# Pre-LN attention and mixture of experts on one core: the next batch's preparation moved into attention, one job queue on a PSUM bank

## The chip, the core and the metric

One core of a Trainium2 chip (8 on the chip, 7 idle). TensorE (PE), VectorE (DVE), ScalarE (ACT), GpSimd (POOL) and SyncE (SP, which here only starts transfers) each run their own instructions in order, and wait for each other by semaphores. The metric is the time of one execution on the device in microseconds, median of several.

## The reference

Four batches of 512 tokens, 128 columns, f32. With x of shape (4, 512, 128), 16 heads of 8 columns, 8 experts of 512 hidden columns:

```python
def attn(x, Wq, bq, Wk, bk):
    q = (x @ Wq + bq).reshape(B, N, 16, 8).transpose(0, 2, 1, 3)
    k = (x @ Wk + bk).reshape(B, N, 16, 8).transpose(0, 2, 1, 3)
    v = k
    a = softmax(einsum('bhnd,bhmd->bhnm', q, k) * 128 ** -0.5)
    return einsum('bhnm,bhmd->bhnd', a, v).transpose(0, 2, 1, 3).reshape(B, N, C)
def ffn(x, w_gate, W1, b1, W2, b2):
    gate = softmax(x @ w_gate.T)
    scores, idx = top_k(gate, 2)
    cw = (one_hot(idx, 8) * scores[..., None]).sum(axis=1)
    h = gelu(einsum('td,edh->teh', x, W1) + b1, approximate=False)
    return einsum('ted,te->td', einsum('teh,ehd->ted', h, W2) + b2, cw)
x = x + attn(layernorm(x), Wq, bq, Wk, bk)
x = x + ffn(layernorm(x), w_gate, W1, b1, W2, b2)
```

## The kernel before

The order of every engine's work is written out by hand: a loop over the batches b, in it 18 attention slots (SLOTS), then the steps of the expert blocks.

*Preparation of a batch.* VectorE takes the moments of the first norm (ln_moments), GpSimd the inverse square root (inv_sqrt), VectorE applies it (ln_apply). TensorE turns x (turn_x), projects it to q and k (project), VectorE adds the bias (add_bias) into qkf. ScalarE (hi_part) and VectorE (lo_part) split q and k into f16 parts side by side in q_aug and k_aug, 32 columns for each head; v_aug holds v and a column of ones. TensorE turns k and q (turn_k, turn_q); ScalarE copies kT (take_kT), VectorE qT0 (take_qT). SP spreads kT into kTm (spread_k), which holds zero outside a head's 32 rows. All of this goes through the PSUM banks SM0 and SM1, which the score maxima use too.

*Attention.* Per head and 128 tokens one matmul of 512 columns gives the scores (score_max, 64 for a batch) and VectorE reduces them to a negative row maximum (row_max), written into q_aug as one more column. For each group of 4 heads q_aug is turned again with the maxima in it (turn_qr, copied by ScalarE in take_qr), and then scores transposed are computed in pairs (score_pair), ScalarE takes the exponential of two banks at once (L575), and values accumulates over 4 slots into bank AV. turn_out turns the result through bank MISC; VectorE divides by the sum and adds x (x1). Slot s holds score pairs of c = s % 4, group s // 4, and the values of slot s - 1. The maxima of batch b are spread: the first `lead(b)` of them (16, 16, 32, 32) before its attention, the others 4 or 3 a slot (sm_of_slot).

*Between attention b and b + 1.* steps(b) steps: for b = 0 there are 9 with no block in them, for b = 1 and 2 the 15 blocks of batch b - 1, for b = 3 the 30 blocks of batches 2 and 3. A block is 128 slots of one expert: up, gelu on ScalarE, down one step later. The steps also hold the end of the preparation of batch b + 1 with its leading maxima, and the routing of batch b: second norm, turned x2, logits (bank AV), top_two, choose, rank_tokens (bank AV), count_blocks, place, name_blocks. Then GpSimd scatters the tokens (scatter, 8 indirect DMAs), SP loads them (load_slots) and the expert's weights (fetch_weights), and at the end GpSimd gathers and VectorE adds (finish).

```python
        def sm_of_slot(b, s):
            rate = 4 if b <= 1 else 3
            first_m = lead(b) + rate * s
            return list(range(first_m, min(first_m + rate, SM_N)))
```

*The order in a slot on TensorE* (L1040 to L1075): one score maximum, turn_k in the last slot, turn_out, score pair 0, one maximum, score pair 1, two maxima, turn_qr in slots 3, 7 and 11, turn_xg and project in slot 15, values, turn_x in 13, project in 14. A score maximum waits for the row maximum two before it (two banks).

*MISC* holds in turn the turned qr, out, x2 and xg; each has semaphores of its own. q_aug, v_aug, qT0 and kTm exist once. On GpSimd the memsets of kTm and v_aug (L396, L397) stand behind the first inv_sqrt, and the memset of xg (L416), for which SP's filling of xs waits (L295), some way behind them. ScalarE splits W1 into two f16 parts in slots 0 to 7 of batch 0 (split_w1), and GpSimd follows (L420).

## Time and profile before

| | us |
|---|---|
| median of 3 runs | 450.85 (450.57 to 451.21) |
| the profiled execution | 453.28 |
| its span, first to last instruction | 451.5 |
| TensorE busy | 375.0 (83%) |
| VectorE busy | 257.0 (57%) |
| ScalarE busy | 244.9 (54%) |
| GpSimd busy | 110.0 (24%) |
| mean granted TensorE clock | 0.906 of 2.4 GHz |

PE is TensorE's matmuls, PEld its weight loads, L878 is line 878 of the kernel. A row in order of time has the start, the duration, the engine, the line, what is written and read with shapes, how many instructions are merged in it (a merged one's duration reaches from the first start to the last end) and, in brackets, how long the engine had been idle and what ended that. Matmuls overlap, so TensorE's cost is read from start to start. The granted clock is 1.00 at 2.4 GHz and 0.50 at 1.2 GHz; in between it is a mean.

### The profile page before, as it was taken

How to read it: one execution, taken by the hardware profiler on the slowest of the kernel's cores; microseconds unless marked ns; L12 is line 12 of the kernel's file. 1: busy time of each engine (PE TensorE's matmuls, PEld its weight loads, DVE VectorE, ACT ScalarE, POOL GpSimd, SP SyncE). 2: the span in 40 equal slices, each digit the busy share in tenths (PEclk: the TensorE clock that was granted, in tenths of full speed). 3: DMA queues.
4: the chain of work that ended last, by engine and by line, in shares of the span. 5: the costliest groups of instructions: out<-in, count | busy, mean ns of one | idle time of the engine just before them, and what ended most of it. 6: DMA issues, size and time to landing. Idle time of an engine off the chain costs nothing. (4 is left out here: it accounts for less than half of the span.)

```text
span 451.5 us, 8146 instructions
## 1 busy us (share of the span) xinstructions
PE 375.0 (83%) x2858; PEld 208.5 (46%) x2858; DVE 257.0 (57%) x607; ACT 244.9 (54%) x322; POOL 110.0 (24%) x112
## 2 busy tenths in 40 slices
PE   3487889775798889979999898899998999989920
PEld 1232223233122224757833235678532358979910
DVE  7677778646877773467768835477678234000202
ACT  1034889870066658723378789233677874444420
POOL 6911331412600000233043001160150003406133
PEclk8556999995589999989999999899999999999975
DMA  5885000002170000324263001341450012576421
GB/s 178 244 272 148 0 1 1 0 14 57 48 245 0 0 1 1 98 100 157 74 197 112 25 1 36 118 169 59 132 202 23 1 54 86 195 267 210 140 83 52
DMA packets 43875, 42.92 MB, mean 95 GB/s; under 512 B 3314, under 2 KB 33082, under 8 KB 43836
## 3 DMA queue, kind: packets, MB, share of 16 engines
q1 hardware_dynamic: 41788, 38.20, 25.7%
q0 software_dynamic: 2048, 4.20, 3.3%
q8 instruction: 25, 0.41, 0.4%
q14 instruction: 14, 0.11, 0.1%
HBM read 11.58 MB, written 11.01 MB: 50 GB/s over the span
## 5 line engine op out<-in xcount | busy, mean ns | idle before, releaser
L659 DVE TENSOR_REDUCE q_aug<-SM 128x1 f16<-128x512 f32 x240 | 156.5, 690 | 50.1 <-PE SM L878 48.9
L575 ACT ACTIVATE probs<-ST 128x1024 f32<-128x1024 f32 x128 | 125.0, 1022 | 31.6 <-PE ST L923 30.4
L878 PE MATMUL SM<-kTm,qT 128*128 128x512 f16 x240 | 94.9, 409 | 18.6 <-DVE q_aug L659 11.4
L514 ACT ACTIVATE hf<-ST 128x512 f32<-128x512 f32 x60 | 35.6, 597 | 85.5 <-PE ST L987 79.9
L923 PE MATMUL ST<-qT,kTm 128*128 128x512 f16 x256 | 76.3, 388 | 4.1 <-ACT probs L575 3.1
L1003 PE MATMUL ST<-w,hf 128*128 x480 | 67.8, 286 | 1.4 <-ACT hf L514 1.4
L936 PE MATMUL AV<-probs,v_aug 128*32 128x512 f32 x512 | 67.5, 604 | 1.0 <-ACT avs L592 0.9
L878 PEld LDWEIGHTS SM<-kTm,qT 128*128 128x128 f16 x240 | 23.9, 99 | 87.7 <-DVE q_aug L659 71.7
L1003 PEld LDWEIGHTS ST<-w,hf 128*128 128x128 f32 x480 | 59.7, 196 | 4.7 <-issue 2.3
L451 POOL DMA_INDIRECT yg<-ys,pos x32 | 32.5, 1015 | 86.7 <-issue 47.8
L387 POOL TENSOR_TENSOR rstd<-ve,neg_half 128x4 f32<-128x4 f32 x8 | 9.3, 1161 | 157.2 <-DVE ve L631 157.2
L987 PE MATMUL ST<-xgT,wblk 128*128 128x128 f16 x240 | 43.8, 221 | 0.0
L986 PE MATMUL ST<-xgT,wblk 128*128 128x128 f16 x240 | 43.8, 221 | 0.0
L985 PE MATMUL ST<-xgT,wblk 128*128 128x128 f16 x240 | 43.8, 221 | 0.0
L923 PEld LDWEIGHTS ST<-qT,kTm 128*128 128x128 f16 x256 | 23.3, 99 | 38.0 <-ACT probs L575 17.1
L439 POOL DMA_INDIRECT xs<-x2s,pos x32 | 31.6, 989 | 36.8 <-DVE pos L719 28.3
L742 DVE SCALAR_TENSOR_TENSOR res<-yg,wgt,x 128x128 f32<-128x128 f32 x16 | 4.5, 345 | 53.0 <-DMA yg<-ys,pos 53.0
L491 ACT ACTIVATE qT<-MISC 128x512 f16<-128x512 f16 x16 | 9.5, 596 | 39.5 <-PE MISC L905 39.2
L986 PEld LDWEIGHTS ST<-xgT,wblk 128*128 128x128 f16 x240 | 23.7, 99 | 7.2 <-issue 0.3
L985 PEld LDWEIGHTS ST<-xgT,wblk 128*128 128x128 f16 x240 | 23.6, 98 | 2.4
L982 PE MATMUL ST<-sel,wblk 128*128 128x512 f16 x60 | 22.9, 382 | 0.9 <-DMA wblk<-wpk 0.4
L987 PEld LDWEIGHTS ST<-xgT,wblk 128*128 128x128 f16 x240 | 23.7, 99 | 0.0
(133 smaller groups left out, 383.9 us busy)
## 6 DMA issues: line engine op xcount, KB each, us to landing
wblk<-wpk SPq DMA_DIRECT2D x60, 288.0 KB
xs<-xg SPq DMA_DIRECT2D x4, 960.0 KB, 7.3
xg<-xs SPq DMA_DIRECT2D x12, 256.0 KB, 3.2
ys<-ysb SPq DMA_DIRECT2D x12, 256.0 KB, 2.4
w<-L_ffn_W SPq DMA_DIRECT2D x1, 2048.0 KB, 11.3
kTm<-kT SPq DMA_DIRECT2D x32, 64.0 KB, 2.0
xt<-L_attn_x SPq DMA_DIRECT2D x4, 256.0 KB, 3.0
out<-res SPq DMA_DIRECT2D x4, 256.0 KB, 2.2
```

Source lines behind the costliest of these rows:

```text
L439: pool.indirect_dma_start(out=xs[b], out_offset=bass.IndirectOffsetOnAxis(ap=pos[:, b, r, t:t + 1], axis=0), in_=x2s[:, t, :, :].rearrange ...
L451: pool.indirect_dma_start(out=yg[:, t, r, :], out_offset=None, in_=ys[f], in_offset=bass.IndirectOffsetOnAxis(ap=pos[:, f, r, t:t + 1], ax ...
L514: act.activation(hf[:, v % HR, :], UP[v % 2], ACT.Gelu, scale=1.0 / WSCALE).then_inc(gelu_done, 1)
L575: act.activation(probs[:, n % 4, :, :], ST[:, n % 2, :, :], ACT.Exp, scale=SCALE).then_inc(exp_done, 1)
L659: dve.tensor_reduce(q_aug[:, m % 4, m // 4, 24:25], SM[m % 2][:, :], AX.X, ALU.max, negate=True).then_inc(sm_max, 1)
L878: pe.matmul(SM[m % 2][:, :], qT0[:, h // 4, P * (m % 4):P * (m % 4) + P], kTm[:, h // 4, h % 4, :], start=True, stop=True).then_inc(sm_ful ...
L923: mm = pe.matmul(ST[:, n % 2, k % 2, :], kTm[:, g, k, P * c:P * c + P], qT1[:, g % 2, :], start=True, stop=True)
L936: last = pe.matmul(AV[32 * j:32 * j + 32, :], v_aug[:, c, 4 * g + j, :], probs[:, (2 * s + j // 2) % 4, j % 2, :], start=(c == 0), stop=(c ...
L985: pe.matmul(col, wb[:, P * c:P * c + P], xgT[:, gq % 2, j, 0, :], start=False, stop=False)
L986: pe.matmul(col, wb[:, P * c:P * c + P], xgT[:, gq % 2, j, 1, :], start=False, stop=False)
L987: last = pe.matmul(col, wb[:, F + P * c:F + P * c + P], xgT[:, gq % 2, j, 0, :], start=False, stop=(c == HC - 1))
L1003: last = pe.matmul(dst, hf[:, v % HR, P * c:P * c + P], w2[:, bass.ds(expert[v], 1), P * c:P * c + P].rearrange("p a n -> p (a n)"), start ...
```

## The change

1. The preparation of batch 1 and 2 runs inside attention 0 and 1 (slots 0 to 12), that of batch 3 begins at the end of attention 1 and runs in the steps after it. steps(0) is 0; routing of batch 0 moves into slots 0 to 8 of attention 1. q_aug, v_aug, qT0 and kTm become double, xt threefold, with the memsets that this takes; other tensors are laid over one another to make room.
2. Everything but the maxima, scores and values goes through MISC, as numbered jobs (misc_order): a job is filled by TensorE (misc_full) when all jobs before it have been emptied (misc_free). The logits and ranks leave AV, x and the projection, k and q leave SM. In a slot the jobs stand between score pair 1 and the third maximum.
3. The row maxima are one stream over all batches: 16 ahead, then 4 a slot in attention 0 and 1 (none in slots 10 and 11 of attention 1), else 2 a slot or step; batch b + 1's follow batch b's without a pause.
4. Order in a slot on TensorE: maximum, pair 0, maximum, pair 1, jobs, maximum, two values, maximum, two values. qr is turned early in slots 3, 7, 11 for b >= 1, last in the slot for b = 0.
5. For batches 1 to 3 the low parts of q and k are formed on GpSimd and not on VectorE; W1 is split in slots 0, 1, 2, 4, 5, 9, 12, 13, the bias later. The rank moves from step 4 to step 5, name_blocks from 5 to 6. The result is written over x1.

```diff
+        LEAD = 16
+        W_SLOTS = (0, 1, 2, 4, 5, 9, 12, 13)
...
         def steps(b):
-            return max(len(blocks_after(b)) + LAG, 9)
+            return len(blocks_after(b)) + LAG if b else 0
...
+        def misc_of_slot(b, s):
+            p = prep_in_att(b)
+            jobs = []
+            if b == 1 and s == 1:
+                jobs.append(("x2", 0))
+            if p is not None and s == 2:
+                jobs.append(("x", p))
+            if s in QR:
+                jobs.append(("qr", b, QR.index(s)))
+            if b == 1 and s == 3:
+                jobs.append(("lg", 0))
+            if p is not None and s in (4, 5):
+                jobs.append(("pr", p, s - 4))
+            if b == 1 and s == 6:
+                jobs.append(("rk", 0))
+            if s == 6:
+                jobs.append(("out", b, 0))
+            if p is not None and s in (8, 9):
+                jobs.append(("k", p, s - 8))
+            if s == 10:
+                jobs.append(("out", b, 1))
+            if p is not None and s in (10, 12):
+                jobs.append(("q", p, (s - 10) // 2))
+            if s == 14:
+                jobs.append(("out", b, 2))
+            if b >= 1 and s == 15:
+                jobs.append(("xg", NQ * (b - 1)))
+            if s == 17:
+                jobs.append(("out", b, 3))
+            if b == 0 and s == 17:
+                jobs.append(("qr", 1, 0))
+            return jobs
...
+        def misc_of_step(b, i):
...
+            if p is not None and i == 0:
+                jobs.append(("x", p))
+            if i == 2:
+                jobs.append(("x2", b))
+            if i == 3:
+                jobs.append(("lg", b))
+            if p is not None and i in (4, 6):
+                jobs.append(("pr", p, (i - 4) // 2))
+            if i == 5:
+                jobs.append(("rk", b))
+            for v in todo[i:i + 1]:
+                gq = group_of(v)
+                if v == group_first(gq) + 1 and v - 1 + group_len(gq) in todo:
+                    jobs.append(("xg", gq + 1))
...
+        def sm_count_slot(b, s):
+            if b == 0:
+                return 4
+            if b == 1:
+                return 0 if s in (10, 11) else 4
+            return 2
+        def sm_count_step(b, i):
+            return 2 if i < NB and b < B - 1 else 0
...
-            pool.memset(kTm[:, :, :, :], 0.0).then_inc(s_kTm, 1)
-            link(pool.memset(v_aug[:, :, :, :], 0.0))
+            pool.memset(kTm[:, 0, :, :, :], 0.0).then_inc(s_kTm, 1)
+            link(pool.memset(v_aug[:, :, :, :, :].rearrange("p a t h r -> p (a t h r)"), 0.0))
...
             pool.memset(xg[:, :, :], 0.0).then_inc(s_zero, 1)
+            pool.memset(kTm[:, 1, :, :, :], 0.0).then_inc(s_kTm, 1)
...
                 for s in range(SLOTS):
+                    early = b >= 1 and s in QR
+                    late = b == 0 and s in QR
+                    sm = sm_slot[b, s]
+                    for bb, m in sm[0:1]:
+                        score_max(bb, m)
+                    if early:
+                        fill_misc(("qr", b, QR.index(s)))
                     if s < 4 * G:
                         score_pair(b, s, 0)
+                    for bb, m in sm[1:2]:
+                        score_max(bb, m)
                     if s < 4 * G:
                         score_pair(b, s, 1)
+                    for job in misc_of_slot(b, s):
+                        if not (s in QR and job[0] == "qr"):
+                            fill_misc(job)
+                    for bb, m in sm[2:3]:
+                        score_max(bb, m)
                     if 1 <= s <= 4 * G:
-                        values(b, s - 1)
+                        values(b, s - 1, 0)
+                    for bb, m in sm[3:4]:
+                        score_max(bb, m)
+                    if 1 <= s <= 4 * G:
+                        values(b, s - 1, 1)
+                    if late:
+                        fill_misc(("qr", b, QR.index(s)))
...
+            def fill_misc(job):
+                pe.wait_ge(misc_free, misc_no[job])
```

## Rows read from the trace of the kernel before

**Rows 1.** Busy time by stage; columns: us, busy (count) of each engine, granted clock, DMA.

```profile
38.03:94.70 56.67, 50.02 (x270) 16.16 (x270) 39.29 (x73) 49.42 (x61) 14.54 (x11) 0.96 0.03 9
94.70:122.76 28.06, 17.56 (x88) 7.85 (x83) 20.52 (x69) 6.24 (x10) 10.51 (x10) 0.60 0.16 47
122.76:181.51 58.75, 52.95 (x306) 18.07 (x305) 39.25 (x79) 39.21 (x48) 1.04 (x1) 0.96 0.14 48
181.51:227.35 45.84, 41.86 (x427) 34.91 (x425) 30.08 (x81) 17.54 (x27) 10.38 (x10) 0.96 0.32 105
227.35:275.96 48.61, 45.39 (x290) 16.41 (x288) 31.32 (x71) 39.67 (x48) 9.18 (x9) 1.00 0.24 78
275.96:321.06 45.10, 41.66 (x427) 34.79 (x425) 30.23 (x82) 17.63 (x28) 10.42 (x10) 0.96 0.30 102
321.06:367.24 46.18, 42.53 (x262) 13.73 (x260) 26.07 (x53) 38.38 (x44) 8.13 (x8) 1.00 0.25 82
367.24:400.69 33.45, 31.74 (x372) 28.71 (x372) 7.73 (x47) 15.38 (x25) 10.08 (x10) 1.00 0.47 162
```

**Rows 2.** Waits over the span: us in total, times, longest us.

```profile
ACT qT L491 <- PE MISC L905: 39.2, 8, 19.0
```

**Rows 3.** Order of time, TensorE, attention 1: start us, us, what.

```profile
130.69 0.39 PE L878 MATMUL SM<-kTm,qT 128*128 128x512 f16 x1
130.92 0.59 PE L923 MATMUL ST<-qT,kTm 128*128 128x512 f16 x2
131.35 0.38 PE L878 MATMUL SM<-kTm,qT 128*128 128x512 f16 x1
...
132.84 1.07 PE L936 MATMUL AV<-probs,v_aug 128*32 128x512 f32 x8
...
133.84 0.39 PE L878 MATMUL SM<-kTm,qT 128*128 128x512 f16 x1
...
138.23 0.39 PE L878 MATMUL SM<-kTm,qT 128*128 128x512 f16 x1
```

**Rows 4.** Order of time, VectorE, attention 1.

```profile
131.12 2.59 DVE L659 TENSOR_REDUCE q_aug<-SM 128x1 f16<-128x512 f32 x4 [0.56 <-PE SM L878]
```

**Rows 5.** Busy time of short stretches that hold one operation or step.

```profile
45.20:46.48 1.28, 1.28 (x12) 0.41 (x5) 0.72 (x2) 1.25 (x3) 0.00 (x0) 1.00 0.00 0
...
147.90:148.72 0.82, 0.82 (x7) 0.31 (x4) 0.75 (x4) 0.00 (x0) 0.00 (x0) 1.00 0.00 0
173.97:174.93 0.96, 0.96 (x8) 0.77 (x5) 0.00 (x0) 0.61 (x1) 0.00 (x0) 1.00 0.00 0
223.81:226.35 2.54, 2.54 (x27) 2.05 (x25) 1.98 (x3) 0.67 (x2) 0.00 (x0) 1.00 0.34 103
356.48:358.45 1.97, 1.97 (x14) 0.47 (x13) 0.00 (x0) 1.97 (x4) 0.00 (x0) 1.00 0.00 0
181.84:183.29 1.45, 1.45 (x27) 1.33 (x25) 1.38 (x10) 1.45 (x2) 0.00 (x0) 1.00 0.05 11
191.32:192.63 1.31, 0.98 (x9) 0.79 (x8) 1.21 (x14) 0.00 (x0) 0.00 (x0) 1.00 0.71 260
194.95:197.07 2.12, 1.20 (x10) 0.97 (x8) 1.81 (x11) 0.41 (x1) 0.00 (x0) 1.00 0.08 29
```

**Rows 6.** Order of time, VectorE and GpSimd, the prelude.

```profile
6.26 8.75 DVE L636 TENSOR_SCALAR xn<-xt,mv,rstd 128x128 f32<-128x128 f32 x2 [0.89 <-POOL rstd L387]
...
16.27 0.69 DVE L671 COPY xT<-SM 128x512 f32<-128x512 f32 x1 [0.57 <-PE SM L837]
...
6.20 6.91 POOL L396 MEMSET kTm<- 128x8192 f16 x1
...
13.06 1.79 POOL L397 MEMSET v_aug<- 128x2048 f32 x1
...
16.53 0.95 POOL L403 MEMSET b2p<- 128x1024 f16 x1
```

**Rows 7.** Order of time, GpSimd, the last blocks.

```profile
380.80 1.08 POOL L439 DMA_INDIRECT xs<-x2s,pos  x1 [6.12 <-DVE pos L719]
```

More of the change, by code:

```diff
@@ L164, in preln_attention_moe @@
         s_bl = sem("s_bl")
-        x_in = sem("x_in")
+        x_in = [sem(f"x_in{b}") for b in range(B)]
         ln_ve = [sem("ln1_ve"), sem("ln2_ve")]
@@ new lines, in misc_of_step @@
+        def misc_of_step(b, i):
+            p = prep_in_steps(b)
+            todo = blocks_after(b)
+            jobs = []
+            if p is not None and i == 0:
[12 more added lines that the diff above has]
+                    jobs.append(("xg", gq + 1))
+            if p is not None and i in (8, 10):
+                jobs.append(("k", p, (i - 8) // 2))
+            if p is not None and i in (11, 12):
+                jobs.append(("q", p, i - 11))
+            if b + 1 < B and i == NB:
+                jobs.append(("qr", b + 1, 0))
+            return jobs
@@ new lines, in preln_attention_moe @@
+        misc_order = [("rows",), ("qr", 0, 0)]
+        for b in range(B):
+            for s in range(SLOTS):
+                misc_order += misc_of_slot(b, s)
+            for i in range(steps(b)):
+                misc_order += misc_of_step(b, i)
+        misc_no = {job: n for n, job in enumerate(misc_order)}
+        def sm_count_slot(b, s):
[6 more added lines that the diff above has]
+            return 2 if i < NB and b < B - 1 else 0
@@ new lines, in preln_attention_moe @@
+        sm_slot, sm_step, m_next = {}, {}, LEAD
+        for b in range(B):
+            for s in range(SLOTS):
+                m_end = min(m_next + sm_count_slot(b, s), B * SM_N)
+                sm_slot[b, s] = [divmod(m, SM_N) for m in range(m_next, m_end)]
+                m_next = m_end
+            for i in range(steps(b)):
+                m_end = min(m_next + sm_count_step(b, i), B * SM_N)
+                sm_step[b, i] = [divmod(m, SM_N) for m in range(m_next, m_end)]
+                m_next = m_end
@@ new lines, in _ @@
+                    early = b >= 1 and s in QR
+                    if s < 4 * G:
+                        weights(b, s, 0)
+                    if early:
+                        empty_misc(("qr", b, QR.index(s)))
+                    if s < 4 * G:
+                        weights(b, s, 1)
+                    for job in misc_of_slot(b, s):
+                        if not (early and job[0] == "qr"):
+                            empty_misc(job)
+                    if prep_in_att(b) is not None and s in (6, 7, 8):
+                        for n in ((0, 1), (2, 3), (4,))[s - 6]:
+                            hi_part(prep_in_att(b), n)
@@ L765, in _ @@
+            for n in range(2):
+                first_qT(n)
+            for m in range(0, LEAD, 2):
                 first_row_max(m)
+            dve.memset(q_aug[:, 1, :, :, :].rearrange("p t h r -> p (t h r)").bitcast(U32), 0).then_inc(s_aug0, 1)
             dve.wait_ge(s_grid, 1)
@@ L961, in turn_xg, with turn_x2, logits @@
                                             xg[:, 4 * q + j, P * a:P * a + P], ident16[:, :])
-                last.then_inc(xg_full, 1)
+                return last
+            def turn_x2(b):
+                for t in range(T):
+                    pe.wait_ge(ln_done[1], T * b + t + 1)
+                    last = pe.transpose(MISC[:, P * t:P * t + P], xn[:, 1, t, :], ident[:, :])
+                return last
+            def logits(b):
+                pe.wait_ge(misc_free, misc_no["x2", b] + 1)
+                for t in range(T):
+                    last = pe.matmul(MISC[:, E * t:E * t + E], x2f[:, P * t:P * t + P], cols[:, :], start=True, stop=True)
+                return last
             expert = {}
@@ L1022, in _ @@
             for _ in range(WARM):
-                pe.matmul(AV[:, :], ident16[:, :], q_aug[:, 0, :, :].rearrange("p h r -> p (h r)"), start=True, stop=True)
-            turn_x(0)
+                pe.matmul(AV[:, :], ident16[:, :], q_aug[:, 0, 0, :, :].rearrange("p h r -> p (h r)"), start=True, stop=True)
+            turn_x(0, SM[0]).then_inc(xT_full, 1)
             pe.wait_ge(s_w, 64)
-            for t in range(T):
-                project(0, t)
+            pe.wait_ge(xT_done, 1)
             for n in range(2):
-                turn_k(0, n)
+                project(2 * n, SM[n])
+                project(2 * n + 1, SM[n]).then_inc(qk_full, 1)
@@ L1030, in _ @@
             for n in range(2):
-                turn_q(0, n)
+                turn_k(0, n, SM16[n]).then_inc(kT_full, 1)
+            for n in range(2):
+                turn_q(0, n, ST16[n]).then_inc(qT_full, 1)
             pe.wait_ge(s_rows, 16)
-            pe.transpose(MISC[:, 0:E], rows[:, :], ident[0:E, 0:E]).then_inc(s_rowsT, 1)
-            for m in range(0, lead(0), 2):
+            pe.transpose(MISC[:, 0:E], rows[:, :], ident[0:E, 0:E]).then_inc(misc_full, 1)
+            for m in range(0, LEAD, 2):
```

682 lines of the change are left out of this document (340 added, 342 removed).

## The prediction

> **What bounds the kernel now.** I read the busy times by stage first, then the waits, then the slots of one attention in order of time. The stages are cut where TensorE begins each one: [rows 1] give TensorE's busy time, its granted clock and the other engines beside it. Attention 0 lasts 56.67 us, then comes a stretch of 28.06 us in which no attention and no expert block runs, then attention 1 (58.75 with its tail), the blocks after it (45.84), attention 2 (48.61), blocks (45.10), attention 3 (46.18), and the last 30 blocks. In most stages TensorE is busy 88 to 95% of the time, so it is the bound. The exception is the stretch of 28.06 us: TensorE is busy 17.56 us of it at a mean granted clock of 0.60 (mostly 1.2 of 2.4 GHz), and ScalarE waits 19.0 us at one go for the first turned q of batch 1 [rows 2]. It is the chain normalise, project, split, turn, sixteen row maxima, and only after it may batch 1 score. That stretch is where the change can win.
>
> Inside an attention the slot is the unit. A regular slot of attention 1 (four score maxima, two score pairs, values) goes from 130.69 to 133.84, so 3.15 us, and the values take 1.00 of it (132.84 to 133.84) [rows 3]. A pair goes from 130.92 to 131.35, so 0.43, and a score maximum is half of it, 0.215. TensorE's work in the slot is 4 x 0.215 for the maxima, 2 x 0.43 for the pairs and 1.00 for the values: 2.72 us. The other 0.43 is waiting. VectorE shows why: four maxima back to back take 2.59, after 0.56 idle [rows 4]. Behind the second pair stand two score maxima in a row, on two PSUM banks, so the second waits for VectorE; then the values keep TensorE for 1.00 and VectorE runs dry. A slot that turns qr goes from 133.84 to 138.23, 4.39 us [rows 3].
>
> **The change part by part.**
>
> *The prelude.* The only edits that matter are on GpSimd: v_aug doubles, so its memset of 1.79 us becomes an estimated 3.6. This is on the path. VectorE's normalisation of batch 0 starts at 6.26 and takes 8.75 us for its first two tiles of 128 columns, where a copy of 512 columns takes 0.69; it ends at 15.0, just after the memsets of kTm (to 13.1) and v_aug (to 14.85) [rows 6]. TensorE's first transposes wait for that, and the filling of xs on SP waits for a later memset in the same queue. Both chains move by 1.8, so the first score maximum starts at 38.03 + 1.8 = **39.8**. The extra x loads and VectorE's memset of the second q_aug I cost at nothing: they stand beside this wait. Cover gone, they cost under 1 us each.
> The new memset of kTm's second half (6.91 us for the first [rows 6]) falls beside the first two copies of qT from PSUM. The nearest row is the copy of xT from PSUM: 0.69 us with a memset running at 16.53 [rows 6], undisturbed. I take 0; if the copies stood until that memset ends, it would be up to 5 us, as the tiles above did. The Trainium skill (SBUF — State Buffer, SBUF: two separate sides) says that GpSimd and a VectorE instruction in a two-port mode, or with two inputs in SBUF, exclude each other for the whole instruction, and (VectorE: DVE Perf Modes, What auto-detection actually checks) that a two-port mode wants source and destination in SBUF. By these pages the norm stands and a copy out of PSUM doesn't, which is the 0 of this point; the rows agree with both.
>
> *Attention 0* now holds 18 x 4 = 72 maxima, the last 24 of them batch 1's, and all of batch 1's preparation. The stretch behind it goes (steps(0) is 0). Spreading the order (maximum, pair, maximum, pair, maximum, half the values, maximum, other half) makes the intervals 0.645, 0.645, 0.715, 0.715: a regular slot becomes 2.72 and VectorE, at 0.645 a maximum, just keeps up. Each job then adds, because it stands between the second and third maximum on both engines and VectorE must wait for TensorE's part:
> - turned output: TensorE 0.43 (an estimate: 512 columns in all, with two passes, no dearer than a pair), VectorE 0.82 [rows 5]; the third maximum ends at 3.4, slot 3.5 (+0.8);
> - projection: TensorE 0.96 [rows 5], then a VectorE add of 0.69, as long as the copy in [rows 6]: slot 3.84; xT or qT: 0.5, then 0.69: 3.3 to 3.36;
> - qr, which in batch 0 stays last in its slot: it waits some 0.4 for the last maximum, and the next pair waits for ScalarE's copy: 4.0 (before 4.39);
> - moments 1.4 (1.38 busy [rows 5]) and an application of the norm 1.1 (an estimate: four tiles at some 0.28), each all VectorE.
> ScalarE's splitting of W1 takes 1.28 a slot [rows 5], beside two exponentials that in a slot without maxima fill 1.97 [rows 5]; spread over eight slots it binds only where k is copied too (slots 8 and 9, together 7.4 with 0.95 for each k).
> Slots 0 and 1 (start at low clock, moments and norm) 9.6; 2: 3.36; 3: 4.0; 4, 5: 7.68; 6: 3.5; 7: 4.0; 8, 9: 7.4; 10 (output and q, each waiting for the other): 4.6; 11: 4.0; 12: 3.3; 13: 2.8; 14: 3.5; 15: 2.8; 16: 2.6; 17 (output, then qr of batch 1): 3.9. Sum **67.0**, against 56.67 + 28.06 = 84.73.
>
> *Attention 1* takes 64 maxima (24 of batch 2), batch 2's preparation and batch 0's routing. Adders: apply, moments of two norms in slots 0 and 1, together 10.4; slot 2: 3.36; slot 3: 5.9, where the logits wait for qr to leave the one bank, which ScalarE does only behind an exponential, and top-two takes 1.31 [rows 5]; slot 4: 4.5; 5: 3.84; 6 (rank, then output; the placing chain is 2.12 [rows 5]): 5.5; 7: 3.4; 8: 3.3; 9: 3.16; 10: 3.55; 11: 2.4; 12: 3.3; 13: 2.72; 14: 3.5; 15: 3.16; 16, 17: 7.7. Sum **69.7**, against 58.75: 11 us dearer. VectorE alone would need about 57 and 60 in the two attentions (72 and 64 maxima at 0.645, with some 10 and 19 us of the other work above), so it is the new bound there.
>
> *Blocks after 1.* A step of three maxima takes 2.54 us with TensorE busy all of it [rows 5]; a third of a maximum's matmul less makes 2.33. 15 x 1.895 + 30 x 0.215 + the jobs (turns, projection, x2, logits 7.3) + 1.6 where the next turned xg waits for VectorE to empty the rank + about 2.4 at the start: **46.0** against 45.84. The preparation of batch 3 has moved in, so nothing is won.
> *Attention 2*: two maxima a slot. 5.6 for the start, 14 x 2.29, jobs 2.8, finish on VectorE 0.8, end 3.5: **44.7** against 48.61. *Blocks after 2*: no preparation: **40.2** against 45.10. *Attention 3*: eight maxima in all; a slot then is 1.97, ScalarE and TensorE both full [rows 5]: 5.5 + 2.3 + 2.6 + 12 x 1.97 + 2.7 for jobs + 2.7 for the end = **39.4** against 46.18.
> *The last blocks.* The scatter of batch 3 starts when the positions are known (380.80 [rows 7]), and the last 15 blocks hang on it through the loads. The rank moves one step later (1.9 less the 0.4 it waited): +1.5, so 33.45 becomes **34.95**. The 50.81 behind 400.69 stay.
>
> Sum: 39.8 + 67.0 + 69.7 + 46.0 + 44.7 + 40.2 + 39.4 + 34.95 + 50.8 = 432.6 us of span, against 451.5. The profiled run took 453.28 and the median is 450.85; scaled by 450.85/451.5 that is **432**.
>
> **The rivals.**
> 1. *The spread order doesn't shorten the slot* (3.15 stays the floor, jobs add to it). For it: latencies between three engines that I have only from one order. It costs 0.43 in some 26 slots, 11 us: **443**.
> 2. *VectorE and TensorE overlap better*: jobs fall into each other's waits, attentions 0 and 1 near VectorE's own 117 us and not 136.7. Half of that gap: **422**.
> 3. *TensorE's clock falls: slower than before.* The forecast has TensorE busy about 52.5 us of 67.0 and of 69.7, lower than the 88% of attention 0 before (clock 0.96) and higher than the 63% of the stretch (0.60) [rows 1]. There it had stood in waits of more than 2 us; now I expect none above 1.4. At 1.2 GHz a slot's 2.72 doubles, some 2.2 us more than my mean slot of 3.8. The gain of 19 us is gone from nine such slots of 36; with half of them it is **470**. The Trainium skill (TensorE: Matmul & The Clock Gate, A second HAM failure mode: psum-queue depth-cycling) reports a kernel whose clock swung because TensorE idled briefly between groups while cycling PSUM banks; by it this would be the outcome. The regular slots of attention 1, with such a pause in each, ran at 0.96, which speaks against.
> 4. *The change doesn't do what it says*: the one bank's order makes batch 1's qr late, so a good part of the 28.06 stays. Each job waits for the one before it; but I count at most two jobs a slot. If 12 us of the stretch stayed: **444**.
>
> **How the numbers follow.** Forecast 0.62 (its own range 425 to 440), rival 1 0.16, rival 2 0.10, rival 3 0.05, rival 4 0.05, the memset beside qT 0.02. The unknown costs (spacing of jobs ±6, last blocks ±1, the memset up to 5) lie in 421 to 446; what is left out is rival 3 and the ends. About 0.2% is what a measurement of this kernel can tell from no change: faster 0.94, same 0.01, slower 0.05.
>
> **What would show it.** Right: batch 1's first exponential near 108 us, no pause between attentions 0 and 1, the next batch's maxima inside attention; regular slots of 2.7 in the middle of attention 1; VectorE busy over 80% in attentions 0 and 1; attention 3's slots at 1.97 to 2.0; VectorE's first norm ending near 16.8. Wrong: slots still 3.15 apart; TensorE waiting on the one bank's copies more than on maxima; a granted clock below 0.9 between 50 and 175 us; a scatter of batch 3 that starts more than 2 us later behind its stage's start.

## The result

The changed kernel takes 469.38 us (median of 4 runs, 467.37 to 470.28); the kernel before, run beside it on the same chip, 451.03. The ratio is 1.039, with a 95% interval of 1.034 to 1.044: slower by 18 us, where 19 us faster was forecast, and outside the range of 421 to 446. The profiled execution took 468.78 us with a span of 467.0, of which TensorE is busy 391.4 (84%).

The stages of the changed kernel, cut where TensorE begins each one as in [rows 1]; columns: us, busy (count) of TensorE, its weight loads, VectorE, ScalarE and GpSimd, granted clock, DMA share, GB/s:

```profile
0.00:42.33 42.33, 19.76 (x74) 9.05 (x75) 29.74 (x36) 6.70 (x10) 28.14 (x28) 0.87 0.77 225
42.33:122.49 80.16, 73.93 (x340) 23.05 (x340) 56.22 (x102) 52.79 (x67) 12.54 (x11) 0.98 0.04 10
122.49:206.95 84.46, 73.64 (x357) 24.08 (x357) 63.16 (x152) 45.19 (x54) 18.72 (x16) 0.98 0.15 49
206.95:252.75 45.80, 42.61 (x451) 36.05 (x452) 31.33 (x85) 19.19 (x31) 12.33 (x12) 1.00 0.29 99
252.75:297.70 44.95, 43.04 (x266) 13.88 (x264) 29.16 (x57) 38.07 (x44) 8.13 (x8) 1.00 0.27 84
297.70:338.94 41.24, 38.16 (x407) 32.49 (x408) 27.82 (x79) 15.03 (x25) 10.08 (x10) 1.00 0.27 98
338.94:380.94 42.00, 37.94 (x238) 11.05 (x236) 10.85 (x29) 37.70 (x44) 8.13 (x8) 1.00 0.29 90
380.94:467.00 86.06, 62.28 (x732) 57.37 (x732) 12.83 (x67) 30.79 (x50) 26.31 (x26) 0.91 0.42 143
```

Beside what the prediction gave for each:

| stage (us) | before | forecast | after | after less forecast |
|---|---|---|---|---|
| to the first score maximum on SM | 38.03 | 39.8 | 42.33 | +2.5 |
| attention 0 (before: and the 28.06 behind it) | 84.73 | 67.0 | 80.16 | +13.2 |
| attention 1 | 58.75 | 69.7 | 84.46 | +14.8 |
| blocks after 1 | 45.84 | 46.0 | 45.80 | -0.2 |
| attention 2 | 48.61 | 44.7 | 44.95 | +0.3 |
| blocks after 2 | 45.10 | 40.2 | 41.24 | +1.0 |
| attention 3 | 46.18 | 39.4 | 42.00 | +2.6 |
| the rest | 84.26 | 85.75 | 86.06 | +0.3 |

The stretch of 28.06 us is gone: attention 1 begins right behind attention 0. Of the miss of 34.4 us, 27.9 lie in these two attentions. TensorE is busy there for 147.6 of 164.6 us, where I had forecast about 105: it isn't waiting, it is busy longer. The group of the values says of what. Here it is on the page of the changed kernel and, below it, on that of the kernel before (line, engine, operation, out<-in, count; busy us, mean ns; idle before, releaser):

```profile
L1117 PE MATMUL AV<-probs,v_aug 128*32 128x512 f32 x512 | 100.9, 610 | 0.0
L936 PE MATMUL AV<-probs,v_aug 128*32 128x512 f32 x512 | 67.5, 604 | 1.0 <-ACT avs L592 0.9
```

The same 512 matmuls of the values kept TensorE 67.5 us before and keep it 100.9 now, at the same mean of one. 512 matmuls of 610 ns each, one after the other, would be 312 us: they overlap, and now they overlap less. TensorE in order of time shows a regular slot of attention 0 (start us, us, engine, line, what; its counterpart before is [rows 3]):

```profile
102.90 0.39 PE L1066 MATMUL SM<-kTm,qT 128*128 128x512 f16 x1
103.12 0.59 PE L1106 MATMUL ST<-qT,kTm 128*128 128x512 f16 x2
103.56 0.38 PE L1066 MATMUL SM<-kTm,qT 128*128 128x512 f16 x1
103.77 0.59 PE L1106 MATMUL ST<-qT,kTm 128*128 128x512 f16 x2
104.20 0.38 PE L1066 MATMUL SM<-kTm,qT 128*128 128x512 f16 x1
104.51 1.05 PE L1117 MATMUL AV<-probs,v_aug 128*32 128x512 f32 x4
105.50 0.39 PE L1066 MATMUL SM<-kTm,qT 128*128 128x512 f16 x1
105.82 1.05 PE L1117 MATMUL AV<-probs,v_aug 128*32 128x512 f32 x4
106.80 0.39 PE L1066 MATMUL SM<-kTm,qT 128*128 128x512 f16 x1
```

Before, `x8` took 1.07 us [rows 3]. Now each `x4`, half of the values, takes 1.05. The slot goes from 102.90 to 106.80, 3.90 us, and no row of it has a wait: two maxima and two pairs take 1.30 (to 104.20), the two maxima ahead of a half 0.31 and 0.32, the halves 0.99 and 0.98.

### The profile page after: what moved, and what is told of

Read it like the earlier page. It is cut to its first block and busy times, and to the rows that moved or that the text cites. A ratio compares the mean times of both kernels' runs of the same rounds, so it can differ in the third digit from the quotient of the medians.

```text
span 467.0 us, 8187 instructions
## 1 busy us (share of the span) xinstructions
PE 391.4 (84%) x2858; PEld 207.0 (44%) x2858; DVE 261.1 (56%) x602; ACT 245.5 (53%) x322; POOL 124.4 (27%) x119
## 5 line engine op out<-in xcount | busy, mean ns | idle before, releaser
L812 DVE TENSOR_REDUCE q_aug<-SM 128x1 f16<-128x512 f32 x240 | 161.2, 691 | 79.3 <-PE SM L1066 77.6
L707 ACT ACTIVATE probs<-ST 128x1024 f32<-128x1024 f32 x128 | 124.5, 1024 | 57.8 <-PE ST L1106 56.6
L1066 PE MATMUL SM<-kTm,qT 128*128 128x512 f16 x240 | 91.5, 387 | 14.9 <-DVE q_aug L812 11.5
L1117 PE MATMUL AV<-probs,v_aug 128*32 128x512 f32 x512 | 100.9, 610 | 0.0
L639 ACT ACTIVATE w<-ST 128x512 f32<-128x512 f32 x60 | 35.8, 597 | 80.8 <-PE ST L1176 80.8
L1192 PE MATMUL ST<-w 128*128 x480 | 66.5, 282 | 0.0
L1066 PEld LDWEIGHTS SM<-kTm,qT 128*128 128x128 f16 x240 | 23.2, 99 | 94.5 <-DVE q_aug L812 68.1
L1192 PEld LDWEIGHTS ST<-w 128*128 128x128 f32 x480 | 58.3, 192 | 3.3
L536 POOL DMA_INDIRECT w<-ys,pos x32 | 32.5, 1015 | 67.3 <-issue 42.6
L1175 PE MATMUL ST<-xgT,wblk 128*128 128x128 f16 x240 | 43.3, 219 | 0.0
L1174 PE MATMUL ST<-xgT,wblk 128*128 128x128 f16 x240 | 43.3, 219 | 0.0
L1176 PE MATMUL ST<-xgT,wblk 128*128 128x128 f16 x240 | 43.3, 219 | 0.0
L1106 PEld LDWEIGHTS ST<-qT,kTm 128*128 128x128 f16 x256 | 22.5, 98 | 39.8 <-ACT probs L707 20.0
L915 DVE SCALAR_TENSOR_TENSOR x<-w,wgt,x 128x128 f32<-128x128 f32 x16 | 4.5, 346 | 55.7 <-DMA w<-ys,pos 55.7
L1117 PEld LDWEIGHTS AV<-probs,v_aug 128*32 128x32 f32 x512 | 14.3, 108 | 28.5 <-issue 22.6
```

Source lines behind the costliest of these rows:

```text
L536: pool.indirect_dma_start(out=yg[:, t, r, :], out_offset=None, in_=ys[f], in_offset=bass.IndirectOffsetOnAxis(ap=pos[:, f, r, t:t + 1], ax ...
L639: act.activation(hf[:, v % HR, :], UP[v % 2], ACT.Gelu, scale=1.0 / WSCALE).then_inc(gelu_done, 1)
L707: act.activation(probs[:, n % 4, :, :], ST[:, n % 2, :, :], ACT.Exp, scale=SCALE).then_inc(exp_done, 1)
L812: dve.tensor_reduce(q_aug[:, b % 2, m % 4, m // 4, 24:25], SM[m % 2][:, :], AX.X, ALU.max, negate=True).then_inc(sm_max, 1)
L1066: pe.matmul(SM[m % 2][:, :], qT0[:, b % 2, h // 4, P * (m % 4):P * (m % 4) + P], kTm[:, b % 2, h // 4, h % 4, :], start=True, stop=True).t ...
L1106: mm = pe.matmul(ST[:, n % 2, k % 2, :], kTm[:, b % 2, g, k, P * c:P * c + P], qT1[:, g % 2, :], start=True, stop=True)
```

## The experiments

The theory: the values of a slot are matmuls of 32 output columns for four heads, and the heads run side by side on TensorE's four column groups. Each head is two matmuls that follow one another on its own group (x8 in all), some 0.5 us each. Taking two heads out of the four then shortens nothing, and a half costs what the whole costs. The rivals: the jobs on the one bank, VectorE, or the order itself set the 3.90.

What eight such matmuls would take one after the other can be read from the projection, which is f32 too but writes all 128 output columns (changed kernel, TensorE; its two products are x4 here, as one head of the values is x2):

```profile
61.51 0.59 PE L1106 MATMUL ST<-qT,kTm 128*128 128x512 f16 x2
61.94 1.03 PE L1032 MATMUL MISC<-wqk,xT 128*128 128x256 f32 x4
62.80 0.38 PE L1066 MATMUL SM<-kTm,qT 128*128 128x512 f16 x1
```

Four matmuls of 256 columns keep TensorE for 0.86 (61.94 to 62.80), 0.215 each. By that a matmul of 512 columns is 0.43, eight in a row would be 3.4, and two in a row 0.86. The values take 1.00 for eight and 0.99 for four: both fit two in a row, with the heads beside each other.

**Both halves together, all else as changed.**

```
-  for bb, m in sm[2:3]:
+  for bb, m in sm[2:4]:
       score_max(bb, m)
   if 1 <= s <= 4 * G:
       values(b, s - 1, 0)
-  for bb, m in sm[3:4]:
-      score_max(bb, m)
-  if 1 <= s <= 4 * G:
       values(b, s - 1, 1)
```

> The changed kernel with one thing put back: TensorE's order behind the second pair is maximum, maximum, both halves of the values, and no longer maximum, half, maximum, half. Nothing is left out of the computation. Theory (a half of the values takes as long as the whole, because the four 32-column groups run side by side): in the changed kernel a half takes 1.05 us and a regular slot of attention 0 and 1 lasts 3.90; with both halves together they take 1.06 in all, and the slot goes back to about 3.15, as in the kernel before, where the second maximum in a row waits about 0.4 for VectorE. Some 30 slots hold four maxima and values, so 30 x 0.75 = about 22 us less: about 447 us. Rival (the jobs on the one bank and VectorE set the slots of 3.9, the order of the values doesn't matter): 467 to 471 us. Second rival (the split costs, but the jobs bind right behind it): 455 to 462 us.

446.16 us (445.45 to 446.62), ratio to the kernel before 0.987 (0.9835 to 0.9904): 23.2 us less than the changed kernel, for a change of order alone. The page's group of the values, and a slot of attention 0 on TensorE and VectorE:

```profile
L1117 PE MATMUL AV<-probs,v_aug 128*32 128x512 f32 x512 | 68.7, 608 | 0.0
```

```profile
93.13 0.39 PE L1066 MATMUL SM<-kTm,qT 128*128 128x512 f16 x1
...
94.44 0.91 PE L1066 MATMUL SM<-kTm,qT 128*128 128x512 f16 x2
95.28 1.06 PE L1117 MATMUL AV<-probs,v_aug 128*32 128x512 f32 x8
96.28 0.39 PE L1066 MATMUL SM<-kTm,qT 128*128 128x512 f16 x1
...
96.70 1.34 DVE L812 TENSOR_REDUCE q_aug<-SM 128x1 f16<-128x512 f32 x2 [0.56 <-PE SM L1066]
```

The values' 32 us are back, and the slot is 3.15 (93.13 to 96.28), as before the change. The two maxima in a row take 0.84 until the values begin, where two cost 0.22 + 0.31 elsewhere: 0.31 is waiting for VectorE, which then runs dry for 0.56 while the values run. Attention 0 and 1 take 67.22 and 73.66 in this kernel. The split cost these two attentions 12.9 and 10.8 us, 23.7 in all. So the theory holds, and the rivals' share is small.

**The converse: the kernel before, with its values split.** (`values` gets a third argument, 0 for the first two heads of a slot and 1 for the last two; that part of the edit isn't shown.)

```
+  if 1 <= s <= 4 * G and sm[3:4]:
+      values(b, s - 1, 0)
   for m in sm[3:4]:
       score_max(b, m)
...
   if 1 <= s <= 4 * G:
-      values(b, s - 1)
+      if not sm[3:4]:
+          values(b, s - 1, 0)
+      values(b, s - 1, 1)
```

> The kernel before with one part of the change alone: the values of a slot that holds four maxima are split around the fourth. 22 slots have both (11 in attention 0, 11 in attention 1). Nothing is left out. Theory (a half costs the whole): TensorE gets 1.0 us more in each of them, of which 0.43 falls into the wait of the second maximum in a row: 22 x 0.6 to 0.75 = 13 to 17 us more, 464 to 468 us. Rival (a half costs half, as the prediction had it): the slot falls from 3.15 to 2.72, 22 x 0.43 = 9 us less, about 442 us.

467.46 us (466.7 to 468.49), ratio 1.0335 (1.0294 to 1.0376): 15.35 us more than before, 0.70 for each of 22 slots. Its page and a slot of attention 1:

```profile
L936 PE MATMUL AV<-probs,v_aug 128*32 128x512 f32 x512 | 91.1, 609 | 0.9 <-ACT avs L592 0.9
```

```profile
137.02 0.39 PE L878 MATMUL SM<-kTm,qT 128*128 128x512 f16 x1 [0.36 <-DVE q_aug L659]
...
138.63 1.05 PE L936 MATMUL AV<-probs,v_aug 128*32 128x512 f32 x4
139.62 0.39 PE L878 MATMUL SM<-kTm,qT 128*128 128x512 f16 x1
139.94 1.05 PE L936 MATMUL AV<-probs,v_aug 128*32 128x512 f32 x4
140.92 0.39 PE L878 MATMUL SM<-kTm,qT 128*128 128x512 f16 x1
```

Busy 91.1 instead of 67.5 us: 23.6 more, 1.07 for each split slot, which is one whole pass of values. The slot lasts 3.90 (137.02 to 140.92), as in the changed kernel. With one part of the change alone, nearly the whole loss is there (0.70 a slot, where the changed kernel lost 23.7 us in 30 slots, 0.79); the numbered queue, the preparation inside attention and the one stream of maxima have no part in it.

**The spread order, with the values whole between the last two maxima.**

```
   if 1 <= s <= 4 * G:
       values(b, s - 1, 0)
+      values(b, s - 1, 1)
   for bb, m in sm[3:4]:
       score_max(bb, m)
-  if 1 <= s <= 4 * G:
-      values(b, s - 1, 1)
```

> The changed kernel with both halves of the values together, and one maximum on each side of them: maximum, pair, maximum, pair, maximum, values, maximum. Nothing is left out. Theory (the spread order was right, only the price of a half was wrong): TensorE's work in a slot is 2.72 us, VectorE at 0.645 a maximum needs 2.59, and two banks let TensorE run ahead by one maximum over the 1.0 of the values; slots of 2.75 to 2.85, so 30 x 1.1 = about 33 us less than the changed kernel: 436 us, and 10 us less than with the two maxima in a row. Rival (three engines' latencies hold the slot at 3.15 whatever the order, rival 1 of the prediction): the same time as with the two maxima in a row, about 447 us.

453.78 us (453.03 to 455.65), ratio 1.0043 (1.0023 to 1.0064). A miss: 18 us above what I expected, and 7.6 above the order with the two maxima in a row. TensorE and VectorE around one slot:

```profile
98.60 0.38 PE L1066 MATMUL SM<-kTm,qT 128*128 128x512 f16 x1
98.91 1.06 PE L1117 MATMUL AV<-probs,v_aug 128*32 128x512 f32 x8
99.90 0.60 PE L1066 MATMUL SM<-kTm,qT 128*128 128x512 f16 x2
...
101.08 0.39 PE L1066 MATMUL SM<-kTm,qT 128*128 128x512 f16 x1
...
100.33 1.89 DVE L812 TENSOR_REDUCE q_aug<-SM 128x1 f16<-128x512 f32 x3 [0.62 <-PE SM L1066]
```

From one third maximum to the next it is 3.15 us again (95.45 to 98.60). VectorE gets one maximum ahead of the values and then waits 0.62 for the next: the values keep TensorE for 0.99, and a maximum can be read only some 0.4 after its matmul starts (99.90 to 100.33), not 0.215. Then VectorE is behind, and TensorE stands 0.29 for a bank (the pair that starts at 100.35 is through at 100.79, the next maximum starts at 101.08). I had reckoned with TensorE one maximum ahead, but the two banks don't give it that. What makes this order dearer than the other at the same regular slot is the jobs: a slot with a turned k lasts 3.28 in e1_whole (75.62 to 78.90) and 3.59 here (78.13 to 81.72). In e1_whole the job's 0.44 lets VectorE catch up ahead of the two maxima in a row, and takes the place of their wait. Here TensorE's wait for a bank lies ahead of the job, where the job can't take its place, and behind the job VectorE is the one that waits (0.38 ahead of the maximum at 82.59); so the job is added whole.

**Halves that really are halves: all four heads, 256 of the 512 columns.**

```
+  if pr == 0 and c == 0:
+      return
...
-  pe.wait_ge(exp_done, PAIRS * b + 2 * s + pr + 1)
-  for j in (2 * pr, 2 * pr + 1):
-      last = pe.matmul(AV[32 * j:32 * j + 32, :], v_aug[:, b % 2, c, 4 * g + j, :],
-                       probs[:, (2 * s + pr) % 4, j % 2, :], start=(c == 0), stop=(c == T - 1))
+  pe.wait_ge(exp_done, PAIRS * b + 2 * s + 2)
+  cs = slice(0, N) if c == 0 else slice(N // 2 * pr, N // 2 * pr + N // 2)
+  for j in range(4):
+      last = pe.matmul(AV[32 * j:32 * j + 32, cs], v_aug[:, b % 2, c, 4 * g + j, :],
+                       probs[:, (2 * s + j // 2) % 4, j % 2, cs],
+                       start=(c == 0), stop=(c == T - 1 and pr == 1))
```

The first of the four accumulating values of a group (c = 0) stays whole, behind all four maxima; so 22 of the 30 slots have halves.

> The changed kernel with the values split by columns instead of by heads: each half holds all four heads (the four 32-column groups) on 256 of the 512 columns, and stands where the changed kernel has its halves (maximum, half, maximum, half); the first of four accumulating values of a group stays whole, behind both maxima. Nothing is left out. Theory (time goes by columns streamed, the four groups run side by side): a half takes 0.5 to 0.6 us, the regular slot 2.72 to 2.85 instead of 3.15 in e1_whole (446.2 us). 22 slots of attention 0 and 1 have both: 22 x 0.35 = 8 us less, about 438 us. This is what the prediction took for granted. Rival (32 x 256 pieces are bound by their weight loads or by the change between tile shapes, each half 0.75 us or more): 446 us or more. Second rival (the spread order gives nothing, as in e2_spread, where VectorE ran dry all the same): 444 to 448 us.

446.96 us (446.31 to 450.77), ratio 0.9908 (0.9882 to 0.9933): no better than e1_whole, and 9 us above my expectation. A slot of attention 0 on TensorE:

```profile
72.06 0.38 PE L1066 MATMUL SM<-kTm,qT 128*128 128x512 f16 x1
72.36 0.64 PE L1120 MATMUL AV<-probs,v_aug 128*32 128x256 f32 x8
72.94 0.39 PE L1066 MATMUL SM<-kTm,qT 128*128 128x512 f16 x1
73.26 0.64 PE L1120 MATMUL AV<-probs,v_aug 128*32 128x256 f32 x8
```

Now a half is nearly a half: 0.58 (72.36 to 72.94) against 1.00. That settles what a half costs, and by which cut. But the slot is 1.31 + 2 x (0.31 + 0.58) = 3.09 with no wait in it, only 0.06 below 3.15; a whole one, from 101.31 to 104.39, lasts 3.08. A maximum (128 output columns) takes 0.22 ahead of a pair and 0.31 ahead of values (32 columns): each change to the other shape costs 0.09, and each separate half 0.08 above its 0.50. It is the shape and not the number format: a pair of f16 takes its usual 0.43 ahead of the f32 projection (61.51 to 61.94 in the rows above). And by the projection's 0.215 for 256 columns, two halves' matmuls in a row are 0.43 and two whole ones 0.86, so a group of values costs some 0.15 on top, long or short (an estimate from these rows). What the spread order saves in waiting, the cuts cost again, and the jobs, as in e2_spread, find no wait to fall into.

Behind these rows stands a page of the Trainium skill (TensorEngine Tiling (Array Packing), Tiling Modes). It lists "128×32: 4 tiles", says that "Different tiles can execute LdWeights and Matmul in parallel", and that a change of tiling mode drains TensorE. The rows agree that the four tiles run their matmuls side by side (x4 and x8 take 1.05 and 1.07 us) and that a change of shape costs something, 0.09; that a drain is the reason, no run here shows. Had I weighed that page against [rows 3], the half would have stood at 1.0 in the sum.

**The start: SyncE copies kT into kTm ahead of the fills of xs.**

```
+  for n in range(2):
+      spread_k(0, n)
   sp.wait_ge(s_zero, 1)
   for b in range(B):
       sp.dma_start(xs[b].rearrange("(j p) c -> p j c", p=P), xg[:, :, :]).then_inc(s_fill, 16)
...
-  for n in range(2):
-      spread_k(0, n)
```

In the changed kernel the first maximum waits for these copies, which stand in the queue behind the fills (SyncE's DMAs, then TensorE):

```profile
25.68 8.95 SPq L362 DMA_DIRECT2D xs<-xg  x4
34.74 8.70 SPq L377 DMA_DIRECT2D kTm<-kT  x8
42.33 0.61 PE L1066 MATMUL SM<-kTm,qT 128*128 128x512 f16 x1 [3.19 <-DMA kTm<-kT]
```

> The changed kernel with SyncE's copies of kT into kTm for batch 0 put ahead of the four fills of xs instead of behind them. Nothing is left out. Theory: the first score maximum waits 3.2 us for these copies (it starts at 42.33), because the fills start 1.7 us later and take 9.0 instead of 7.7, and the copies then take 8.7 instead of 6.9. Ahead of the fills they are done before the maxima of VectorE's first round end, so the first maximum starts near 39.2 and the kernel is 3 us faster: about 466.3 us. Rival (the fills then collide with something later, or the wait only moves to q's copy or the low clock): 469 us, no change.

466.26 us (464.85 to 467.03), 3.1 less than the changed kernel, and its first maximum starts at 39.65, 2.7 earlier. (The kernel before, run beside each round, was 451.03 beside the changed kernel and 452.11 beside this one; against it the gain is nearer 4.) With half of v_aug's memset moved behind the other memsets as well, on e1_whole:

```
-  link(pool.memset(v_aug[:, :, :, :, :].rearrange("p a t h r -> p (a t h r)"), 0.0))
+  link(pool.memset(v_aug[:, 0, :, :, :].rearrange("p t h r -> p (t h r)"), 0.0))
...
   pool.memset(kTm[:, 1, :, :, :], 0.0).then_inc(s_kTm, 1)
+  link(pool.memset(v_aug[:, 1, :, :, :].rearrange("p t h r -> p (t h r)"), 0.0))
+  pool.memset(v_aug[:, 1, :, :, :].rearrange("p t h r -> p (t h) r")[:, :, 8:9], 1.0).then_inc(s_aug_v, 1)
```

> e1_whole (446.2 us) with the start mended: SyncE's copies of kT ahead of the fills of xs (3.1 us less in the run where that was done alone), and the second half of v_aug set to zero by GpSimd only behind the other memsets. Nothing is left out. Theory: VectorE's first normalisation stands until GpSimd's memsets of kTm and v_aug end; with half of v_aug it ends 1.7 us earlier, and everything of the start moves by that: 446.2 - 3.1 - 1.7 = 441.4 us. Rival (the normalisation is bound by something else, its two tiles only happen to end with the memset): 443 us.

440.53 us (439.66 to 442.3), 5.6 below e1_whole. VectorE's normalisation follows the memset:

```profile
6.43 9.44 DVE L776 TENSOR_SCALAR xn<-xt,mv,rstd 128x128 f32<-128x128 f32 x4 [0.90 <-POOL rstd L456]
```

It took 10.97 us in e1_whole with the memset of all of v_aug (3.50 us), and takes 9.44 with half (1.79). The first maximum starts at 37.44, where in e1_whole it is 42.47.

**GpSimd's two subtractions for the biases, moved off batch 2's normalisation** (on e1_whole).

```
   rest_x2(0)
-  rest_bias()
   lo_part(2, 0)
   lo_part(2, 1)
+  pool.wait_ge(aug_lo, 6)
+  rest_bias()
   scatter_all(0)
```

In the changed kernel, attention 1 has this in slot 1 (VectorE, GpSimd, TensorE):

```profile
132.23 3.69 DVE L774 TENSOR_SCALAR xn<-xt,mv,rstd 128x128 f32<-128x128 f32 x2
131.63 2.12 POOL L506 TENSOR_TENSOR wpk<-wblk 4x1024 f16<-4x1024 f32 x1 [0.17 <-POOL x2s L514]
133.72 2.12 POOL L508 TENSOR_TENSOR b2p<-wblk 1x1024 f16<-1x1024 f32 x1
135.98 0.84 PE L1027 MATMUL MISC<-ident,xn 128*128 128x128 f32 x3 [1.70 <-DVE xn L774]
137.42 1.92 PE L1117 MATMUL AV<-probs,v_aug 128*32 128x512 f32 x4
```

Two tiles last 3.69 us, to the end of GpSimd's second subtraction; TensorE waits 1.70, and its next half of values takes 1.92 instead of 1.05: over 137.40 to 141.20 the granted clock is 0.55, near the lower of its two levels (1.2 of 2.4 GHz).

> The changed kernel with both halves of the values behind the last maximum (as in e1_whole, 446.2 us) and, new, GpSimd's two subtractions for the biases (2.22 and 2.12 us) moved behind the low parts of batch 2, out of the time in which VectorE normalises batch 2. Nothing is left out. Theory (the two engines exclude each other when both read SBUF only): in e1_whole the four tiles of that normalisation take from 118.73 to 123.4 instead of 1.1 us, and the pieces behind it run at half clock; without the overlap about 3.5 us less, and up to 1.5 more if the clock doesn't fall: 441 to 443 us. The scattering of batch 0 starts 4 us later, which its reader has room for. Rival (VectorE waits there anyway, or the scatter's delay reaches the blocks): 446 us, no change.

440.68 us (440.55 to 440.93), 5.5 less than e1_whole. All four tiles take 1.10 us, the subtractions now start at 147.06, and attention 1 lasts 68.81 instead of 73.66:

```profile
118.62 1.10 DVE L775 TENSOR_SCALAR xn<-xt,mv,rstd 128x128 f32<-128x128 f32 x4
```

Part of this is the clock, and that part isn't safe, as e9_best shows below.

**All together.**

> All three together: values split by columns in the spread order, the start mended, the biases' subtractions moved. Nothing is left out. If the parts add up: 438 - 4.8 - 3.5 = about 430 us; the forecast for the change was 432. If the overlap of jobs, clock and waits eats a part of it: 433 to 437 us.

441.17 us (440.1 to 441.48): a miss by 11. Some 6 of it are the split by columns, which brings nothing: e6_columns less the two gains of 5.6 and 5.5 would be 435.9. The other 5.3 stay open. Against e9_best (below), whose values alone stand otherwise, its profiled execution is 1.7 us longer in attentions 0 and 1 (68.86 and 70.84) and 1.4 in the last stage. With the values whole behind the two maxima in a row instead:

> The changed kernel with three things mended: both halves of the values together behind the last maximum (446.2 us alone), the start (5.6 us less), the biases' subtractions off the normalisation (5.5 us less). Nothing is left out. If the parts lie in different stages and add up: 446.2 - 5.6 - 5.5 = 435 us, a ratio of 0.963 to the kernel before. If a part of them is given back where batch 1's chain now waits for something else: 437 to 440 us.

436.76 us (435.26 to 438.79), ratio 0.9666 (0.9632 to 0.9699): 15 us below the kernel before, 1.7 more than the sum of the parts. Its attentions 0 and 1:

```profile
37.33:105.01 67.68, 59.19 (x343) 20.75 (x341) 56.21 (x107) 52.59 (x68) 12.54 (x11) 0.97 0.16 43
105.01:175.31 70.30, 59.10 (x357) 22.18 (x357) 58.06 (x152) 44.73 (x54) 18.74 (x16) 0.98 0.18 59
```

The stages behind them are those of the changed kernel within 0.4 us.

Attention 1 takes 70.30 here and 68.81 in e5_rest_bias. The difference is the clock in slots 1 and 2. The next kernel, e10_rank, is the same program up to the last stage, and TensorE has the same waits in both ahead of slot 1's values, to 0.01 us (1.11, 0.21, 0.21, 1.67 and 0.21, all for VectorE). But the values right behind them run at the lower clock in the first of these two rows (e9_best) and not in the second (e10_rank):

```profile
113.31 1.94 PE L1120 MATMUL AV<-probs,v_aug 128*32 128x512 f32 x8
113.20 1.07 PE L1120 MATMUL AV<-probs,v_aug 128*32 128x512 f32 x8
```

From the first pair of slot 1 to that of slot 3 it is 10.68 us in e9_best (109.01 to 119.69; granted clock 0.83, then 0.86), 9.16 in e10_rank and 9.17 in e5_rest_bias (1.00 in both). So 1.5 us, most of the 1.7 above the sum of the parts, hang on whether the clock falls behind the same waits, and these runs don't show what decides it.

**Batch 3's rank one step earlier** (on e9_best).

```
-  if i == 5: jobs.append(("rk", b))
+  if i == (4 if b == B - 1 else 5): jobs.append(("rk", b))
...
-  if i == 6: name_blocks(b)
+  if i == (5 if b == B - 1 else 6): name_blocks(b)
```

> e9_best with batch 3's rank of the tokens one step of the blocks earlier (the fifth step instead of the sixth), and the naming of its blocks with it. Nothing is left out. Theory (the prediction costed this move at 1.5 us: the last 15 blocks hang on the scatter of batch 3, which starts when the positions are known): in the changed kernel the choice is ready at 391.05 and the rank starts at 392.61, so it can come 1.5 to 1.6 us earlier, and the end with it: 433.4 us. Rival (the end hangs on TensorE or on the weights of the last blocks, not on the scatter): 435 us, no change.

434.24 us (432.91 to 436.66), ratio 0.9611 (0.958 to 0.9642), the lowest median of all, 2.5 us below e9_best. But the runs of the two overlap (435.26 to 438.79 there), and the profiled executions don't show the gain at the end (GpSimd, TensorE):

```profile
361.51 1.08 POOL L526 DMA_INDIRECT xs<-x2s,pos  x1 [6.33 <-DVE pos L897]
378.65 1.01 PE L1138 MATMUL MISC<-ident,xg 128*128 128x128 f16 x8 [2.13 <-DMA xg<-xs]
```

The scatter starts 13.84 us behind the stage's start (347.67), where in e9_best it is 15.08: 1.24 earlier. But TensorE then waits 2.13 for the loads and takes 1.01 for the turns, at the lower clock (0.61 for the same eight at 2.4 GHz), and the stage to the end lasts 86.93 against 86.38. The profiled execution is 1.1 us shorter in all, for it reaches that stage 1.65 earlier, 1.5 of which is the clock in attention 1, which this edit doesn't touch. So the scatter does start earlier, but that the kernel gains by it isn't shown.

## Why the prediction was wrong, step by step

*What bounds the kernel now.* The reading of the stages held. The reading of the slot held one number that was taken for something it is not: the values' 1.00 us stood in the row as `x8` with 1.07, and the page gave 604 ns as the mean of one matmul. I read 1.00 as the sum of eight pieces, to be cut anywhere. That records overlap doesn't yet show that they run side by side: the eight f16 turns of k, 219 ns each, overlap too, and their 0.45 (75.62 to 76.07 in e1_whole) is about what 1024 f16 columns take one after the other (0.43, two maxima). What does show it stood in the prediction itself: the projection, 512 f32 columns in all, at 0.96, and the values, 4 x 512 f32 columns, at 1.00.

*The step that failed* is in "Attention 0": "maximum, half the values, maximum, other half makes the intervals 0.645, 0.645, 0.715, 0.715: a regular slot becomes 2.72". The half was put at 0.50; it is 0.99. The slot became 3.90. That is 1.18 above the forecast in a regular slot, and 30 slots of the two attentions hold four maxima and values. Putting the halves together took 23.2 us off, and splitting them in the kernel before, in 22 slots, added 15.35. This is the whole sign of the result. The two attentions missed by 27.9 us: the split accounts for 23.7 (by e1_whole), and 4.9 are the norm of the paragraph on attention 1 (by e5_rest_bias, with what the clock did there); the rest together came in 0.7 under the forecast. It isn't 30 x 1.18, since only regular slots were forecast at 2.72: slots 8 and 9, with a turned k each, took 8.70 together (80.66 to 89.36), 1.3 above their 7.4. No rival of mine had it: I looked for what could wait, not for work that could grow.

*A second error, which the first hid.* Even with a cut that halves the time, 2.72 isn't to be had: the maxima ahead of values cost 0.31 and not 0.215, and a separate half 0.58. Rival 1 (3.15 stays the floor) was right in its size: three orders gave 3.15, 3.15 and 3.09. I gave it 0.16.

*The sum of attention 0 and 1 as repaired* (67.68 and 70.30 in e9_best, 67.0 and 69.7 forecast) looks like a hit and isn't one. TensorE is busy for 118.3 us in them, not 105. The regular slot is 0.43 dearer than forecast, and the jobs are cheaper, for they fall into the wait ahead of the second maximum in a row: slots 8 and 9 took 6.55 together in e1_whole (75.62 to 82.17), where 7.4 was forecast.

*Attention 1* had one more error of 5 us: an application of the norm at 1.1, beside which the diff moves GpSimd's two subtractions. The rule that I used for the memset beside qT (GpSimd and a two-port instruction of VectorE exclude each other) applied here, and I didn't ask it of this pair. The Trainium skill (SBUF — State Buffer, SBUF: two separate sides) has it, and the rows agree: 3.69 us for two tiles beside the subtractions, 1.10 for four without. Rival 3's mechanism showed in small: after the wait of 1.70 us, values at the lower clock. Its place and price didn't: the clock is 0.98 over both attentions. Its sum had a slip, too: 2.72 doubled is 5.44, 1.6 above the mean slot of 3.8 and not 2.2, so half of the slots would give 462 and not 470.

*The prelude.* The memset came as forecast (3.50 us against 3.6), and so did the 0 for the memset of kTm beside the copies of qT: each takes 0.69 while that memset runs. The step "the first score maximum starts at 38.03 + 1.8" missed 2.5 us, because both chains were moved by the same 1.8 without looking at what stands between them: the kTm copies wait in SyncE's queue behind the fills, and both took longer (8.95 and 8.70 us, where the trace of before has 7.70 and 6.92). Why they did stays open.

*The blocks and attention 2* came within 1.0 us (the terms for the blocks after 1 add up to 46.2, not 46.0). *The rank's delay* came as forecast: batch 3's scatter starts 15.10 behind the stage's start (396.04), where before it was 13.56, so 1.5 later. *Attention 3*: the slot of 1.97 held (350.96 to 352.93), but four slots with their turned q and output last 9.49 (350.43 to 359.92), 1.6 above 4 x 1.97; three such groups are 4.8 us, where I had 2.7 for jobs.

*Rival 4* is out: the first exponential of batch 1 is at 123.35, 0.86 behind the start of attention 1, and TensorE's waits ahead of all jobs on the one bank are 6.9 us over the two attentions (from the groups of its lines in that stretch).

Of the signs that I named, "slots still 3.15 apart" was meant as the worst case; the real ones were 3.90 with TensorE busy through. The sign to ask for was TensorE's busy time in a slot.

## What to carry to other kernels

Before you cut a group of matmuls in two, compare its time from start to start with what as many matmuls of its format and columns take in a row that is known to run one after the other (here 0.43 each, from the projection; 1.00 for eight of the values). Where the group is much shorter, its members run side by side. A cut between them then saves nothing, and both parts together take twice the time; a cut along the streamed columns nearly halves each part (here 0.58 of 1.00). Count times mean is no yardstick, since records overlap in plain rows too. Changes between tile shapes cost too (0.09 us here), so an order that alternates them must save more waiting than it adds switches. And when work of one engine is moved, ask of every pair that now meets whether the two exclude each other, not only of the pair that you noticed.

## What the runs showed of the hardware

- Matmuls of 32 output columns on four column groups: four (two heads) take 1.05 us, eight (four heads) 1.07; with 256 instead of 512 columns eight take 0.64.
- A 128-column matmul takes 0.22 us ahead of another such and 0.31 ahead of a 32-column one.
- Two f32 products of 256 columns on all 128 output columns (x4) take 0.86 us, one after the other; the values' 4 x 512 columns take 1.00.
- Behind the same five waits of TensorE (the longest 1.67 us) the granted clock fell to 0.83 over slot 1 in e9_best and stayed at 1.00 in e10_rank; it cost 1.5 us.
- VectorE begins on a score maximum 0.42 us after its matmul starts (96.28 to 96.70 in e1_whole), though TensorE goes on to the next after 0.22; so with two banks VectorE runs dry for 0.56 to 0.62 us over the values in either order.
- A subtraction of GpSimd on 4 partitions, or on only 1, takes 2.12 us for 1024 elements, where one on 128 partitions with 512 takes 1.16: 2.1 and 2.3 ns for each element of a partition, so the few partitions save nothing. VectorE's normalisation, beside them, doesn't end before the second does (135.92 and 135.84).
